# First layer: latents of all tiles from turned rows kept on chip, then the gates beside the latents' norm

## The reference

```python
q = _rmsnorm(x @ wq_a.T, q_a_ln_w) @ wq_b.T                     # 128 latents -> 32 heads x 128
ckv, k_pe = split(x @ wkv_a.T)                                   # 32 latents and 64 rotary columns
kv = _rmsnorm(ckv, kv_a_ln_w) @ wkv_b.T                          # keys 64, values 128 a head
...                                                              # rotary, causal softmax, values
s = out @ wo.T

q = x[:, 107:255, :].mean(axis=1)                                # token mean of an entry
routing = softmax(q @ router_W.T + router_b)                     # 8 experts
t = einsum('bsd,erd->bser', x, A)                                # rank 16 each
g = x @ W.T + b + einsum('bser,eor,be->bso', t, B, routing) * 2
```

## Time and profile before

| what | us |
| --- | --- |
| median of 3 runs (1585.55 to 1586.72) | 1586.24 |
| the profiled execution | 1587.04 |
| its span, first to last instruction | 1585.2 |

### The profile page before, as it was taken

One profiled execution on the slowest core, in us unless ns is written; L12 is line 12 of the kernel. 1 busy time (PEld: TensorE's weight loads), 2 busy tenths in 40 slices (PEclk: granted clock), 3 DMA queues, 4 the chain that ended last, 5 costly groups with the idle time before them and its releaser, 6 DMA issues. The chain is left out here.

```text
span 1585.2 us, 25823 instructions
## 1 busy us (share of the span) xinstructions
PE 1404.6 (89%) x8210; PEld 1143.0 (72%) x8211; DVE 752.0 (47%) x1723; ACT 560.1 (35%) x1743; POOL 622.0 (39%) x521
## 2 busy tenths in 40 slices
PE   3999789999999999999996685999999999999950
PEld 0566467777777777777763485999999999999940
DVE  5221466666666666666665674222222222222227
ACT  0232245555555555555553243112111112112114
POOL 0000234444444444444444366534446254471035
PEclk9899989999999999999998897999999999999985
DMA  8032200000000000000003775545656455564337
GB/s 274 0 107 87 100 14 1 14 14 13 13 14 13 13 13 13 13 13 13 14 21 134 291 266 186 190 144 177 211 175 236 141 186 187 183 231 139 106 112 253
DMA packets 66558, 171.50 MB, mean 108 GB/s; under 512 B 6000, under 2 KB 14592, under 8 KB 66192
## 3 DMA queue, kind: packets, MB, share of 16 engines
q0 software_dynamic: 25712, 97.94, 18.5%
q1 hardware_dynamic: 35040, 62.39, 11.8%
q10 hardware_dynamic: 5760, 10.57, 1.9%
...
## 5 line engine op out<-in xcount | busy, mean ns | idle before, releaser
L1593 PE MATMUL bank<-expert_weights,rows_t 128*128 x1872 | 358.7, 347 | 10.6 <-DVE rows_t L1519 10.6
L1593 PEld LDWEIGHTS bank<-expert_weights,rows_t 128*128 128x128 f32 x1872 | 340.3, 189 | 14.2 <-issue 11.0
L926 POOL TENSOR_TENSOR room<-room 128x1024 f32<-128x1024 f32 (+1 forms) x128 | 187.7, 1466 | 343.2 <-DVE room L837 343.2
L896 ACT ACTIVATE room<-bank,room 128x256 f32<-128x256 f32 (+1 forms) x512 | 207.9, 420 | 131.2 <-DVE room L822 131.0
L696 PE MATMUL bank<-room 96*128 (+2 forms) x1024 | 232.4, 347 | 0.3
L1531 DVE TENSOR_TENSOR x_keep<-x_keep,bank 128x400 f32<-128x400 f32 x78 | 44.5, 571 | 303.2 <-ACT x_keep L1470 301.8
L1025 POOL TENSOR_TENSOR expert_weights<-x_keep,expert_weights 128x1600 fp32r<-128x1600 f32 (+2 forms) x49 | 160.2, 3270 | 49.4 <-DMA expert_weights<-w 49.2
L696 PEld LDWEIGHTS bank<-room 96*128 96x128 f32 x1024 | 156.4, 192 | 28.0 <-issue 1.6
L1616 PE MATMUL bank<-expert_weights,act_t 128*128 x702 | 165.6, 389 | 1.0 <-ACT act_t L1475 1.0
L1616 PEld LDWEIGHTS bank<-expert_weights,act_t 128*128 128x128 f32 x702 | 131.5, 188 | 25.6 <-issue 1.3
L1470 ACT ACTIVATE x_keep<-bank 128x400 f32<-128x400 f32 x78 | 39.3, 504 | 298.0 <-PE bank L1593 298.0
...
## 6 DMA issues: line engine op xcount, KB each, us to landing
...
room<-wo SPq DMA_DIRECT2D x16, 512.0 KB, 5.2
```

The source lines that it names most:

```text
L896: last = sc.activation(Pr[:, m % 4, hh, 0:w], scores_bank(m)[:, w * hh:w * hh + w], ACT.Exp, bias=nb[:, par, hh:hh + 1], scale=SCALE, accu ...
L926: g.tensor_tensor(pr, pr, rs[:, one[1] % 2].unsqueeze(2).broadcast_to([P, 4, w]), ALU.mult).then_inc(normed, 1)
L1593: last = mm(psum(2 * hf + w)[:, 0:HF], xgT[:, par, of_x, P * k:P * k + P], W[:, ds(off + (of_w * SLOT + (k * 2 + w) * FF + hf * HF), HF)], ...
```

## The change

`first_projections` and `normalise_latents` become one function and one block, `first_stage`, in two passes over the tiles.

- Pass 1 does, per tile: turn, latents, lora-a. The turned tile goes to `XNT`, which keeps all 16 tiles; XN becomes a ring of four. x comes in nine groups (1, 1, and seven of 2). ACT copies latents and lora-a out of PSUM, the lora part unscaled. The two folds of wq follow tiles 8 and 11.
- Token means are sums that DVE takes over the turned tiles; the mean matmuls and their constants go. The factor 1/148 is applied to the logits.
- Between the passes: router, softmax, root of the latents' variances. DVE then scales the lora parts in place, two tiles at a time.
- Pass 2 does, per tile: gate base, gate lora, and the fold of wo after every second tile. The normalised latents are turned on PE after tiles 4 (queries) and 7 (keys). Gates go through a ring of three tiles with one semaphore each; the waits for their stores stand in attention, on ACT behind its prologue and on SP.
- The loads are in another order: wqkv and lora-a behind the first tile of x on SP, the other weights on POOL's queue behind the eighth tile. Some of them share memory with Wo, so the first fold of wo waits until the remainder of the rotary query weights has been taken.
- In attention SCALE moves into the copy of the keys; the maxima are negated in the reduction itself, so L822 and its semaphore go, and the exponentials need no scale.

```diff
...
+    GROUPS = ((0, 1), (1, 2)) + tuple((t, t + 2) for t in range(2, NT, 2))
+    LASTG = len(GROUPS) - 1
+    FOLD_AFTER = (8, 11)
...
+            bring_x(0)
+            sp.dma_start(s.ident, a["consts"][:, 0:LAYER1_AT]).then_inc(ident_in, 16)
+            sp.dma_start(wqkv, a["wqkv"]).then_inc(qkv_w_in, 16)
+            sp.dma_start(A, a["lora_a"]).then_inc(qkv_w_in, 16)
+            for g in range(1, 4):
+                bring_x(g)
+            sp.dma_start(wqn[0:NOPE], a["wq_nope"]).then_inc(fold_q_in, 16)
+            sp.dma_start(wkb[0:NOPE], a["wkv_k"]).then_inc(fold_q_in, 16)
+            for g in range(4, len(GROUPS)):
+                bring_x(g)
+            sp.dma_start(s.vecs[:, :], a["vecs"].broadcast_to([P, D + QR + KVR + NE])).then_inc(consts_in, 16)
+            sp.dma_start(s.C[:, :], a["consts"][:, LAYER1_AT:LAYER2_AT]).then_inc(consts_in, 16)
+            bring_wo(0)
+            bring_wo(1)
+            for i in range(NB):
+                if i + 1 < NB:
+                    sp.wait_ge(foldo, i + 1)
+                    bring_wo(2 * i + 2)
+                    bring_wo(2 * i + 3)
+                keep_gate(2 * i)
+                keep_gate(2 * i + 1)
...
+            pool.wait_ge(x_in[4], 16)
+            pool.dma_start(rW, a["router"]).then_inc(router_in, 16)
+            pool.dma_start(W, a["gate_w"]).then_inc(gate_w_in, 16)
+            pool.dma_start(B, a["lora_b"]).then_inc(lora_b_in, 16)
+            pool.dma_start(rope_raw, a["wq_rope"]).then_inc(rope_in, 16)
+            pool.dma_start(wvb, a["wkv_v"]).then_inc(fold_v_in, 16)
...
+            pool.wait_ge(consts_in, 32)
+            pool.wait_ge(qka_out, NT)
+            pool.wait_ge(foldq, 2)
...
+            def latents_leave(t):
+                ps = psum(2 + t % 2)
+                act.wait_ge(lo_done, t + 1)
+                sc.activation(QKA[:, t], ps[:, 0:QKW], ACT.Copy).then_inc(junk_done, 1)
+                junks.n += 1
+                sc.activation(tT[:, t], ps[:, 256:256 + P], ACT.Copy).then_inc(qka_out, 1)
+                junks.wait()
+                junks.then(sc.activation(junk, QKA[:, t, 0:QR], ACT.Square, accum_out=s.ss[:, t, 0:1]))
+                junks(sc.activation(junk[:, 0:KVR], QKA[:, t, QR + ROPE:QKW], ACT.Square, accum_out=s.ss[:, t, 1:2]))
...
+            root_of(0)
+            root_of(1)
+            turn_out(0)
+            root_of(2)
+            for t in range(NT):
+                if t + 1 < NT:
+                    if t >= 1 and t % 2 == 1 and t // 2 + 3 <= LASTG:
+                        root_of(t // 2 + 3)
+                    turn_out(t + 1)
+                latents_leave(t)
+                if t in FOLD_AFTER:
+                    fold_q_leaves(FOLD_AFTER.index(t))
...
+            act.wait_ge(var_ready, len(GROUPS) + 2)
+            sc.activation(root, var, ACT.Sqrt).then_inc(std_ready, 1)
+            act.wait_ge(mix, MAXED)
+            sc.activation(ex[0:NB], lg[0:NB], ACT.Exp, bias=m8[0:NB], accum_out=sm8[0:NB]).then_inc(mix, 1)
+            act.wait_ge(rope_in, 16)
+            sc.activation(wq[:, HIGH, :, 0:ROPE], rope_raw, ACT.Copy).then_inc(wq_high, 1)
+            for t in range(NT):
+                act.wait_ge(gate_out, t + 1)
+                sc.activation(G[:, t % GATE_BUFS], G[:, t % GATE_BUFS], ACT.Silu).then_inc(silu_done, 1)
+                if t % 2 == 1:
+                    fold_leaves(t // 2)
+                if t == 4:
+                    for g in range(4):
+                        act.wait_ge(lat_turned, g + 1)
+                        sc.activation(s.QAT[:, 4 * g:4 * g + 4], psum(g).rearrange("p (t n) -> p t n", t=4),
+                                      ACT.Copy).then_inc(qat_out, 1)
...
+            def mean_of(t):
+                lo, hi = (MEAN_FROM, P) if t % 2 == 0 else (0, MEAN_TO - P)
+                dve.wait_ge(turned_out, t + 1)
+                step(v.tensor_reduce(part[:, t], XNT[:, t, :, lo:hi], AX.X, ALU.add))
...
+                for t in range(t0, t1):
+                    if t >= XN_BUFS:
+                        dve.wait_ge(turned, t - XN_BUFS + 1)
+                    v.tensor_scalar(XN[:, t % XN_BUFS], X[:, t], mv[:, t, 0:1], rs[:, t:t + 1], ALU.subtract,
+                                    ALU.mult).then_inc(xn_ready, 1)
+                if g >= 3:
+                    for t in range(*GROUPS[g - 3]):
+                        mean_of(t)
+            for g in range(LASTG - 2, LASTG + 1):
+                if g == LASTG - 1:
+                    dve.wait_ge(consts_in, 32)
+                    v.tensor_copy(s.identb[:, :], ident)
+                    v.tensor_copy(s.maskb[:, :], const("causal"))
+                    for f in range(2):
+                        dve.wait_ge(wq_high, f + 1)
+                        v.tensor_tensor(wq[:, LOW, 16 * f:16 * f + 16, ROPE:KC],
+                                        psum(4 + f).rearrange("p (h c) -> p h c", h=16),
+                                        wq[:, HIGH, 16 * f:16 * f + 16, ROPE:KC], ALU.subtract).then_inc(wq_low, 1)
+                for t in range(*GROUPS[g]):
+                    mean_of(t)
+            step.wait()
+            by_entry = part.rearrange("p (b two) k -> p two b k", two=2)
+            v.tensor_tensor(qmT.rearrange("p k b -> p b k"), by_entry[:, 0], by_entry[:, 1], ALU.add).then_inc(mix, 1)
+            dve.wait_ge(junk_done, 3 * NT)
+            v.tensor_scalar(var[:, :, 0], s.ss[:, :, 0], 1.0 / QR, RMS_EPS, ALU.mult, ALU.add).then_inc(var_ready, 1)
+            v.tensor_scalar(var[:, :, 1], s.ss[:, :, 1], 1.0 / KVR, RMS_EPS, ALU.mult, ALU.add).then_inc(var_ready, 1)
+            dve.wait_ge(mix, LOGITS)
+            step.then(v.scalar_tensor_tensor(out=lg[0:NB], in0=psum(7)[0:NB, 64:64 + NE],
+                                             scalar=1.0 / (MEAN_TO - MEAN_FROM), in1=rbias, op0=ALU.mult, op1=ALU.add))
+            step.then(v.tensor_reduce(m8[0:NB], lg[0:NB], AX.X, ALU.max))
+            v.tensor_scalar(m8[0:NB], m8[0:NB], -1.0, None, ALU.mult).then_inc(mix, 1)
+            dve.wait_ge(std_ready, len(GROUPS) + 1)
+            rsqrt_refined(v, step, rr, root, var)
+            v.tensor_copy(root, rr).then_inc(rr_ready, 1)
+            dve.wait_ge(mix, EXPS)
+            step.then(v.reciprocal(sm8[0:NB], sm8[0:NB]))
+            step.then(v.tensor_scalar(lg[0:NB], ex[0:NB], sm8[0:NB], LORA_SCALE, ALU.mult, ALU.mult))
+            v.tensor_copy(rexp[0:NB], lg[0:NB].unsqueeze(2).broadcast_to([NB, NE, RANK])).then_inc(mix, 1)
+            def q_group(g):
+                part_ = QKA[:, 4 * g:4 * g + 4, 0:QR]
+                step.then(v.tensor_tensor(part_, part_, rr[:, 4 * g:4 * g + 4, 0:1].broadcast_to([P, 4, QR]), ALU.mult))
+                v.tensor_tensor(part_, part_, qln.unsqueeze(1).broadcast_to([P, 4, QR]), ALU.mult).then_inc(q_ready, 1)
+            def scale_lora(b):
+                two = tT[:, 2 * b:2 * b + 2]
+                v.tensor_scalar(two, two, rt[:, b:b + 1], None, ALU.mult).then_inc(scaled, 1)
+            def fold_rest(i):
+                dve.wait_ge(foldo_out, i + 1)
+                v.tensor_tensor(s.Wo[:, LOW, i], psum(6 + i % 2), s.Wo[:, HIGH, i], ALU.subtract).then_inc(foldo_low, 1)
+            dve.wait_ge(mix, RT_PS)
+            step.then(v.tensor_copy(rt, psum(7)[:, 128:128 + NB]))
+            dve.wait_ge(qka_out, NT)
+            for b in range(NB):
+                scale_lora(b)
+            q_group(0)
+            dve.wait_ge(wq_high, 3)
+            v.tensor_tensor(wq[:, LOW, :, 0:ROPE], rope_raw, wq[:, HIGH, :, 0:ROPE], ALU.subtract).then_inc(wq_low, 1)
+            for t in range(NT):
+                dve.wait_ge(gate_done, t + 1)
+                if t >= GATE_BUFS:
+                    dve.wait_ge(s.gates_stored[t % GATE_BUFS], 16 * (t // GATE_BUFS))
+                v.tensor_tensor(G[:, t % GATE_BUFS], psum(4 + t % 2), bias, ALU.add).then_inc(gate_out, 1)
+                if 0 < t < 4:
+                    q_group(t)
+                if t % 2 == 0 and t:
+                    fold_rest(t // 2 - 1)
+                if t == 8:
+                    for g in range(4):
+                        dve.wait_ge(lat_turned, 4 + g + 1)
+                        v.tensor_scalar(s.KT[0:KC, 512 * g:512 * g + 512], psum(g)[0:KC], SCALE, None, ALU.mult)
+            fold_rest(NB - 1)
...
+            pe.wait_ge(ident_in, 16)
+            turn(0)
+            for t in range(NT):
+                if t + 1 < NT:
+                    turn(t + 1)
+                if t == 0:
+                    pe.wait_ge(qkv_w_in, 32)
+                pe.wait_ge(turned_out, t + 1)
+                if t >= 2:
+                    pe.wait_ge(qka_out, t - 1)
+                ps, xT = psum(2 + t % 2), XNT[:, t]
+                for k in range(4):
+                    mm(ps[:, 0:QKW], xT[:, k], wqkv[:, k], start=(k == 0), stop=(k == 3))
+                for k in range(4):
+                    last = mm(ps[:, 256:256 + P], A[:, k], xT[:, k], start=(k == 0), stop=(k == 3))
```

(68 more changed lines are left out.)

434 lines of the change are left out of this document (122 added, 312 removed).

## The result

The changed kernel takes 1532.82 us (median of 4 runs, 1530.12 to 1534.1) beside 1585.98 of the kernel before in the same set: ratio 0.9662, 95% interval 0.9645 to 0.9679. The forecast was 1544.6, its range 1533 to 1558: faster was right, the size was not, and the time lies 0.2 us under the range. The two profiled spans are 1531.1 and 1585.2, 54.1 us apart.

What follows compares the result with a forecast made beforehand. PE's early start, work per tile, the hole of the latents' norm and attention's waits bound the kernel; 36.9 + 0.7 + 4.0 = 41.6 us off the profiled 1587.04 gave 1545.4, as median 1544.6 us, range 1533 to 1558.

Steps and rivals of the forecast that it cites:

- attention's: Attention's 128 steps: dropping the 226 ns multiply of the maxima shortens PE's waits for POOL's product; 4 us gained, bounds 0 to 10.
- Pass 1: Turn, latents and lora-a of all tiles, 2.87 us a tile, plus folds and low clock behind them; ends at 76.1 us.
- Middle: Between the passes: DVE's short operations held by POOL, PE idle, one clock fall; base 2 at +19.7, effectively +22.2 = 98.3 us.
- Pass 2: Gates and folds of wo: seven pairs at 9.67 us plus 3.6 of transposes; last fold ends at 169.6, attention starts at 171.5.
- rival D: The two sets of latents' transposes lower the clock, 2.5 us each: 1549.6 us; chance 0.04.
- Prologue: Start of attention: PE comes warm instead of after 20 us of low clock; 0.7 us gained, bounds 0 to 1.5.
- ACT's new waits: Waits for stored gates in attention come after or beside 15 us of its prologue; cost 0.
- A: No clock falls behind the folds and in the middle; 7.5 us less, 1537.1 us; chance 0.12.
- B: Pass 1 is paced by PE waiting for ACT's turn copy, 3.6 us a tile; 1555.6 us; chance 0.14.
- C: The norm is moved, not hidden: POOL holds DVE through the middle, base 2 at +32; 1554.6 us; chance 0.07.
- E: Attention's shortened chain pays in all 45 waits for POOL's product; 6 us less, 1538.6 us; chance 0.07.
- F: Transfers of wo and gates pace pass 2; at 15 us landing a pair takes 16.9, 1595 us; chance 0.02.

Runs made afterwards that it cites:

- e4: The changed kernel with the multiply by -SCALE back in attention's chain, but on ACT instead of DVE; ratio 0.9681 to the kernel before.
- e1: The changed kernel with the old attention step: DVE multiplies the maxima by -SCALE again and the exponentials take the scale; ratio 0.9757 to the kernel before.
- e3: The changed kernel with a multiplication that nobody reads added on DVE right behind the reduction of the maxima; ratio 0.9736 to the kernel before.
- e10: The changed kernel with a small reduction that nobody reads added on DVE behind the reduction of the maxima; ratio 0.9733 to the kernel before.
- e6: The changed kernel with the two folds of wq cut into eight pieces of four heads, behind tiles 4 to 11; ratio 0.9643 to the kernel before.
- e12: The changed kernel with wq's folds in eight pieces, ACT's gate waits one query copy earlier and POOL's keys behind DVE's wq rope remainder; ratio 0.961 to the kernel before.
- e15: The changed kernel with wq's folds moved into the middle and ACT's gate waits one tile of queries earlier; ratio 0.9602 to the kernel before.

## Why the prediction was wrong in size, step by step

By the spans the sum was 41.6 us and 54.1 were measured. Of the 12.5 between them attention's loop is 11.5, the first stage 5.0 (41.9 for 36.9), the prologue -1.7 and the later stages -2.3.

**The failed term is attention's: 4 us predicted, 15.5 measured**, over its upper bound of 10. The prediction followed the multiplication along "chain maxima, exponentials, product" and took less than half of 45 waits by 0.23 us. That chain is worth about 3 to 4 us (e4 4.0; e1 less e3, 586.7 - 583.8 = 2.9), which is what was priced, though by a share of the waits that was a guess. What it left out is DVE's queue: the multiplication also stood ahead of the rotary operations and of the reciprocal that releases POOL's product. That costs 13.6 us (e3), of which 9.0 even for an operation that is never held (e10). The two, 4.0 and 13.6, are more than the 16.5 of both together (e1, 586.7 for 570.2), since each hides some of the other. The row said where the waits were, but its mean of 226 ns against a median of 170 should have raised the question of what held it (the second number here), and the order on DVE was not read.

```profile
L822 DVE TENSOR_SCALAR room<-room x128: 169/170/634, 226.1 to 836.4; 128x4 f32<-128x4 f32 x128
```

**Pass 1: 76.1 predicted, 72.09 measured.** Start 13.6 for 14.6; first tile 3.57 for 4.8, because the clock rose within it; folds 4.19 + 3.75 = 7.9 for 9.1; low clock behind them 2.75 + 1.7 = 4.45 for 5.0 (e6 takes it away and gains 3.0). Tiles 2.84 apart for 2.87. The mechanism was right, with three terms some 1 us too dear each and one 0.5. The start and the first tile (2.2 us together) are within what one trace differs from another, so that part may be luck.

**Middle: +18.8 for +19.7.** Right in its causes: DVE held by POOL, PE idle behind it, one fall of the clock (base 2 at 5.45 for 3.60, and fold 0 at 1.94 for 1.06, 2.7 us together for 2.5). PE idled 6.0 us and not some 8. The copy of the factors ended at +10.7 and not +12.8, since only four of the short operations were held for long.

**Pass 2.** From base 2 to the end of the last fold 163.54 + 1.07 - 90.91 = 73.7 us; predicted 71.3 and 2.5 for the fall, 73.8. The transposes lie in stretches at clock 1.00 (107 to 109 above, and 123 to 128), so rival D did not come, and the rule of the Trainium skill's page TensorE: Matmul & The Clock Gate, section Part 4: PE-mode transpose, that transposes are no activity for the clock, is not contradicted by two sets of 1.7 us between full matmuls; it shows only that sets this short did no harm here. Attention 1.9 us later: 166.5, predicted 171.5.

**Prologue**: 0.7 gained was predicted, 1.0 lost. Both parts of this failed. PE did not come warmer than before: in stretches of 2 us from attention's start the granted clock is 1.00, 0.79, 0.50, 0.86 before and 1.00, 0.76, 0.50, 0.89 now. And ACT's new waits were priced at nothing behind "15 us of cover"; the cover was there for the stores, but they moved the table load behind the first maxima, which costs 1.1 (e12 and e15 move it back and take 22.4 and 22.3 us).

**Rivals.** A (no falls) is refuted, its time of 1537 still too slow. B (hand-overs pace pass 1) failed: 2.84 a tile, no wait on ACT. C failed with base 2 at +18.8. E named the place but by the wrong path and with 10 us as its ceiling. F (transfers pace pass 2) failed: wo landed in 5.8 us, gates in 6.2, no wait of PE in pass 2, and a ring of two did not change the ratio.

Wo's landing time (5.8 for 5.2) and x not being a pace stand as predicted. Later stages differ by 2.3 us between the two traces, for which no step of the change is a cause that I can show.
